# A gated cross-attention stack: first-attention scores in four row groups, biases folded, one-operation rounding

## The reference

```python
x = x + tanh(g_xattn[0]) * L0_xattn(layernorm(x), ctx)   # 16 heads of 16, softmax over 361 context rows, then W1, relu, W2
x = x + tanh(g_ffn[0])   * L0_ffn(layernorm(x))          # top-1 mixture of 8 experts
x = x + tanh(g_xattn[1]) * L1_xattn(layernorm(x), ctx)   # ternary weights, int8 activations
x = x + tanh(g_ffn[1])   * L1_ffn(layernorm(x))          # 16 experts project q, k, v; attention inside each batch
```

## Time and profile before

| what | us |
|---|---|
| median of three runs (lowest, highest) | 641.66 (640.87, 642.61) |
| the profiled execution's own time | 640.18 |
| its span | 638.4 |
| PE busy in the span | 591.8 (93%) |
| DVE busy | 325.1 (51%) |
| ACT busy | 219.7 (34%) |
| POOL busy | 72.1 (11%) |

### The profile page before, as it was taken

One profiled execution on the slowest core, in us unless ns is written; L12 is line 12 of the kernel. 1 busy time (PEld: TensorE's weight loads), 2 busy tenths in 40 slices (PEclk: granted clock), 3 DMA queues, 4 the chain that ended last, 5 costly groups with the idle time before them and its releaser, 6 DMA issues.

```text
span 638.4 us, 9303 instructions
## 1 busy us (share of the span) xinstructions
PE 591.8 (93%) x3611; PEld 393.6 (62%) x3611; DVE 325.1 (51%) x772; ACT 219.7 (34%) x511; POOL 72.1 (11%) x69
## 2 busy tenths in 40 slices
PE   6989999999999889999998399777899999999996
PEld 4756444444556769999996267547465555555653
DVE  3696767588668451121221877777742223222542
ACT  2644655646663461112214454482210000000100
POOL 0053200000008011223221000000100100000000
PEclk9999999999999878999999699886999999999999
DMA  8900000100003634999991000600633743230000
GB/s 203 344 17 1 16 2 1 35 2 3 1 2 101 217 112 164 328 338 361 322 358 61 22 0 1 232 2 0 198 108 99 265 140 96 78 99 1 0 27 26
DMA packets 25195, 69.93 MB, mean 110 GB/s; under 512 B 5143, under 2 KB 12919, under 8 KB 21319
## 3 DMA queue, kind: packets, MB, share of 16 engines
q1 hardware_dynamic: 21798, 58.16, 27.6%
q0 software_dynamic: 3360, 11.28, 5.2%
HBM read 64.62 MB, written 4.80 MB: 109 GB/s over the span
## 4 chain that ended last, share of the span: by engine, by line
PE 87%; DVE 5%; ACT 3%; DMA 2%; issue 1%; POOL 1%; SPq 0%; DVEq 0%; ACTq 0%; POOLq 0%
PE bank L2035 20%; PE bank L1559 12%; PE bank L1877 8%; PE bank L1890 8%; PE bank L1706 7%; PE bank L2071 7%; PE bank L1680 5%; PE bank L1724 3%; PE bank L1934 2%; PE bank L1649 2%; PE bank L1957 2%; PE bank L1712 2%; ACT region L1458 1%; PE bank L1960 1%; PE bank L1947 1%
## 5 line engine op out<-in xcount | busy, mean ns | idle before, releaser
L2035 PE MATMUL bank<-region,kvT 128*128 128x400 f32 x384 | 130.4, 500 | 1.0 <-DVE region L1138 1.0
L2035 PEld LDWEIGHTS bank<-region,kvT 128*128 128x128 f32 x384 | 72.4, 190 | 55.5 <-issue 1.6
L1144 DVE TENSOR_TENSOR region<-xT,stage 128x800 f32<-128x800 f32 x30 | 29.7, 992 | 69.7 <-PE bank L2035 69.5
L714 DVE TENSOR_REDUCE nmax<-bank 100x2 f32<-100x722 f32 x64 | 55.2, 905 | 15.1 <-PE bank L1680 14.7
L1877 PEld LDWEIGHTS bank<-stage,region 128*128 128x128 f32 x448 | 54.7, 200 | 1.6 <-issue 0.9
L1877 PE MATMUL bank<-stage,region 128*128 128x128 f32 x448 | 55.0, 283 | 0.5 <-ACT stage L1393 0.5
L1890 PE MATMUL bank<-region,stage 128*128 128x256 f32 x224 | 50.7, 379 | 0.0
L1890 PEld LDWEIGHTS bank<-region,stage 128*128 128x128 f32 x224 | 41.5, 190 | 5.1
L2071 PE MATMUL bank<-region,kvt 128*128 128x400 f32 x128 | 43.9, 500 | 0.0
L916 DVE TENSOR_SCALAR stage<-bank,stage 128x128 f32<-128x128 f32 x56 | 15.8, 344 | 52.0 <-PE bank L1877 52.0
L1706 PE MATMUL bank<-xT,kvt 64*121 64x400 f32 (+1 forms) x144 | 38.9, 543 | 1.5 <-ACT kvT L1372 0.6
(11 more groups left out here) (337 smaller groups left out, 899.9 us busy)
## 6 DMA issues: line engine op xcount, KB each, us to landing
region<-in_e_w SPq DMA_DIRECT2D x28, 1024.0 KB, 5.2
kvT<-in_p_qkv SPq DMA_DIRECT2D x32, 384.0 KB, 3.1
stage<-w_dram POOLq DMA_DIRECT2D x2, 1600.0 KB, 12.9
stage<-in_t_f SPq DMA_DIRECT2D x1, 2048.0 KB, 14.7
kvt<-in_p_o SPq DMA_DIRECT2D x1, 2048.0 KB, 8.8
stage<-in_e_b SPq DMA_DIRECT2D x14, 128.0 KB, 7.2
region<-in_ctxT SPq DMA_DIRECT2D x3, 541.5 KB, 13.5
stage<-w_dram POOLq DMA_DIRECT2D x1, 1200.0 KB, 9.4
```

Source lines behind the costliest of these rows:

```text
L714: dve.tensor_reduce(nmax[:, b % 2, at_h:at_h + 9:8], banks[0:N, bank:bank + 2, 0:M], AX.X, ALU.max, negate=True)\
L1144: dve.tensor_tensor(x_w[n % NW], xT[:, :, at_h], w_bc[h][:, None, e, :].to_broadcast([P, 2, HT]), ALU.mult).then_inc(S["xw_done"], 1)
L2035: ins = pe.matmul(psum[3 * h + j][:, 0:HT], p_w[n % NP][:, k, j * HE:(j + 1) * HE], x_w[n % NW][:, k, :], start=e == 0 and k == 0, stop=e ...
```

## The change

It has five parts.

1. **Scores in quads.** The six pairs of a batch become three *quads*, `score_quad(n, c)`: first four bf16 matmuls of 32 rows and 400 columns that add the maxima (L1756 of the changed kernel), then twice four f32 matmuls of 32 rows and 200 columns (L1760), two heads to a row group. `qm` has half the columns, and POOL writes 400 elements a partition instead of 800.
2. **Banks.** Waves and quads take four banks each from a ring of six (banks 0 to 5). `bank_pair_free` makes a group wait, two banks at a time: the second two wait for the first two of the group just before it (for a wave its first reduce, for a quad its second exponential). nm and all chain units share one bank (6), and each waits until ACT has emptied the one before.
3. **Order.** The table `STEP` sets it for PE and ACT: wave 3 is now last but the turn, and wave (n+1, 0) stands behind nm(n), not ahead of it.
4. **Biases.** b_att is folded into the bias of the text layer and into the sum of the two halves, so L1960 is gone, and so are DVE's reciprocal and two products for its row; three small DVE operations are new. 
5. **f2 and a context layer.** One operation scales an input and adds 128, and its write to bf16 rounds it (DVE takes 5 and 3 of the 8 blocks, ACT the others); PE takes 128 times the sum of the weights off again with one more matmul a batch, for which DVE sums the f2 weights behind the expert loop. Context layer 5 is moved ahead of the expert loop.

```diff
-OWN = (0, 3, 6)
+OWN = (5, 3)
+OFFSET = 128.0
...
-FIRST = [0]
-UNIT, CHAIN, TOTAL = {}, {}, {}
-TOP_TURN, TOP_SPREAD, LARGE_SUM = (3, 5), (3, 9), (4, 7)
+CHAIN_BANK, RING = 6, 6
+STEP = (("nm",), ("wave", 0), ("chain", 0), ("quad", 0), ("heads",), ("chain", 1), ("wave", 1), ("chain", 2),
+        ("values", 0), ("quad", 1), ("chain", 3), ("wave", 2), ("chain", 4), ("values", 1), ("quad", 2),
+        ("chain", 5), ("wave", 3), ("turn",))
+TOP_TURN, TOP_SPREAD, LARGE_SUM = (3, 2), (3, 5), (4, 3)
...
+def ring_bank(g, i):
+    return (4 * g + i) % RING
...
-                pool.tensor_tensor(qm[b % 3], qT[:, :, None, b * N:(b + 1) * N].to_broadcast([P, 2, 4, N]),
-                                   const("quadmask")[:, None, :, None].to_broadcast([P, 2, 4, N]),
+                pool.tensor_tensor(qm[b % 3], qT[:, :, None, b * N:(b + 1) * N].to_broadcast([P, 2, 2, N]),
+                                   const("pairmask")[:, None, :, None].to_broadcast([P, 2, 2, N]),
                                    ALU.mult).then_inc(S["qm_done"], 1)
...
                     dve.wait_ge(S["x_mm"], 2 * (4 * b + w) + h + 1)
-                    at_h = 4 * (w % 2) + 2 * h + w // 2
-                    bank = 2 * h + (4 if b == 0 else 0)
-                    dve.tensor_reduce(nmax[:, b % 2, at_h:at_h + 9:8],
+                    bank = 2 * h + 4 if b == 0 else ring_bank(GROUP["wave", b, w], 2 * h)
+                    dve.tensor_reduce(nmax[:, b % 2, 4 * w + 2 * h:4 * w + 2 * h + 2],
                                       banks[0:N, bank:bank + 2, 0:M], AX.X, ALU.max, negate=True)\
                         .then_inc(S["x_max"], 1)
...
+            dve.tensor_scalar(scol[:, 34:35], att[:, 1:2], -0.2, None, ALU.mult)
+            link(dve.tensor_tensor(scol[:, 31:32], att[:, 0:1], att[:, 1:2], ALU.add))
+            dve.scalar_tensor_tensor(scol[:, 32:34], scol[:, 31:32].to_broadcast([P, 2]), 0.1,
+                                     cols[:, COLS["txt"]:COLS["txt"] + 2], ALU.mult, ALU.add)
...
-            dve.wait_ge(S["consts_in"], 16)
-            link(dve.reciprocal(v_scale[:, 2:4], scol[:, 43:45]))
-            for a in range(2):
-                ins = dve.tensor_scalar(bias_row[0:1, a * P:(a + 1) * P], rows[0:1, 512 + a * P:512 + (a + 1) * P],
-                                        v_scale[0:1, 2 + a:3 + a], None, ALU.mult)
-            ins.then_inc(S["v_scale"], 1)
...
+            dve.memset(offset, -OFFSET)
+            link(dve.tensor_reduce(f2_total, weight("f2").rearrange("p (k n) -> p n k", k=8), AX.X, ALU.add))
+            dve.tensor_copy(f2_sum, f2_total).then_inc(S["f2_sums"], 1)
...
-                                  cols[:, 14 + m:15 + m], ALU.mult, ALU.add).then_inc(S["f_out"], 1)
+                                  scol[:, 32 + m:33 + m], ALU.mult, ALU.add).then_inc(S["f_out"], 1)
...
-                dve.tensor_tensor(fsum[:, at_b], fT[:, 0, at_b], fT[:, 1, at_b], ALU.add).then_inc(S["fsum_done"], 1)
+                dve.scalar_tensor_tensor(fsum[:, at_b], fT[:, 0, at_b], scol[:, 34:35], fT[:, 1, at_b], ALU.add, ALU.add)\
+                    .then_inc(S["fsum_done"], 1)
...
                 at_h = slice(h * HT, (h + 1) * HT)
-                if m in OWN:
-                    link(dve.tensor_scalar(h1T[:, m, at_h], h1T[:, m, at_h], scol[:, 23:24], None, ALU.mult))
-                else:
-                    dve.wait_ge(S["act_scaled"], 2 + 5 * h + len([k for k in range(m + 1) if k not in OWN]))
-                dve.tensor_scalar(q1T[:, m, at_h], h1T[:, m, at_h], MAGIC, MAGIC, ALU.add, ALU.subtract)\
+                dve.tensor_scalar(q1T[:, m, at_h], h1T[:, m, at_h], scol[:, 23:24], OFFSET, ALU.mult, ALU.add)\
                     .then_inc(S["q1_done"], 1)
...
+
+            def quad_out(n, c):
+
+                rows_c, g = CH[c][1], GROUP["quad", n, c]
+                for i in range(4):
+                    act.wait_ge(S["y_mm_a"], UNIT[n, c, i] + 1)
+                    act.activation(probsT[n % 2][0:rows_c, c, i].rearrange("p w n -> p (w n)"),
+                                   psum[ring_bank(g, i)][0:rows_c, 0:4 * N], ACT.Exp).then_inc(S["y_out_a"], 1)
...
-            for b in range(5):
+            for b in range(6):
                 last_context_out(b)
...
             for h in range(2):
-                for m in range(8):
-                    if m not in OWN:
-                        act.mul(h1T[:, m, h * HT:(h + 1) * HT], h1T[:, m, h * HT:(h + 1) * HT], scol[:, 23:24])\
-                            .then_inc(S["act_scaled"], 1)
+                at_h = slice(h * HT, (h + 1) * HT)
+                for m in range(OWN[h], 8):
+                    act.activation(q1T[:, m, at_h], h1T[:, m, at_h], ACT.Identity, bias=scol[:, 35:36],
+                                   scale=scol[:, 23:24]).then_inc(S["act_scaled"], 1)
...
-                pe.wait_ge(S["y_out_a"], y - 2)
+                pe.wait_ge(S["y_out_a"], LAST_CHAIN[y] + 1)
                 for k in range(2):
-                    ins = pe.matmul(psum[4 + y % 3][:, 0:M], w[:, k, m * P:(m + 1) * P], qc[0:rows_k, k, b, :],
+                    ins = pe.matmul(psum[CHAIN_BANK][:, 0:M], w[:, k, m * P:(m + 1) * P], qc[0:rows_k, k, b, :],
                                     start=k == 0, stop=k == 1)
                 ins.then_inc(S["y_mm_a"], 1)
...
+            def bank_pair_free(g, e):
+
+                pair = 2 * g + e - RING // 2
+                if pair < 0:
+                    return
+                kind, b, at_u = USER[pair // 2]
+                if kind == "wave":
+                    pe.wait_ge(S["x_max"], 2 * (4 * b + at_u) + pair % 2 + 1)
+                else:
+                    pe.wait_ge(S["y_out_a"], UNIT[b, at_u, 2 * (pair % 2) + 1] + 1)
+
...
+                    if b == 0:
+                        bank = 4 + i
+                        if (w, i) == (1, 2):
+                            pe.wait_ge(S["sum_read"], 1)
+                        if w > 0 and i % 2 == 0:
+                            pe.wait_ge(S["x_max"], 2 * (w - 1) + i // 2 + 1)
+                    else:
+                        bank = ring_bank(GROUP["wave", b, w], i)
+                        if i % 2 == 0:
+                            bank_pair_free(GROUP["wave", b, w], i // 2)
...
-            def score_pair(b, u):
-
-                c, t = u // 4, u // 2 % 2
-                (c0, rows_c), y0 = CH[c], UNIT[b, u]
-                bank = [psum[4 + (y0 + g) % 3][0:rows_c, 0:4 * N] for g in range(2)]
-                for g in range(2):
-                    if y0 + g >= 3:
-                        pe.wait_ge(S["y_out_a"], y0 + g - 2)
-                    at_g = slice(64 * g, 64 * g + 64)
-                    pe.matmul(bank[g], kT[at_g, t, b, c0:c0 + rows_c],
-                              qm[b % 3][at_g, t].rearrange("p j n -> p (j n)"), start=True, stop=False)
-                if u == 0:
+            def score_quad(b, c):
+
+                (c0, rows_c), g = CH[c], GROUP["quad", b, c]
+                bank = [psum[ring_bank(g, i)][0:rows_c, 0:4 * N] for i in range(4)]
+                if c == 0:
                     pe.wait_ge(S["y_out_a"], FIRST[b] + 1)
-                for g in range(2):
-                    at_g = slice(64 * g, 64 * g + 64)
-                    pe.matmul(bank[g], rows_bf[at_g, t, 0:rows_c], nmT[b % 2][at_g, :],
-                              start=False, stop=True).then_inc(S["y_mm_a"], 1)
+                for i in range(4):
+                    if i % 2 == 0:
+                        bank_pair_free(g, i // 2)
+                    at_i = slice(32 * i, 32 * i + 32)
+                    pe.matmul(bank[i], rows_bf[at_i, 0:rows_c], nmT[b % 2][at_i, :], start=True, stop=False)
+                for t in range(2):
+                    for i in range(4):
+                        at_i = slice(32 * i, 32 * i + 32)
+                        ins = pe.matmul(bank[i][:, 2 * N * t:2 * N * t + 2 * N], kT[at_i, t, b, c0:c0 + rows_c],
+                                        qm[b % 3][at_i, t].rearrange("p j n -> p (j n)"), start=False, stop=t == 1)
+                        if t == 1:
+                            ins.then_inc(S["y_mm_a"], 1)
...
+            pe.wait_ge(S["x_max"], 8)
+            for n in range(B):
+                for kind, *at_u in STEP:
+                    if kind == "nm":
+                        turn_maxima(n)
+                    if kind == "wave" and n + 1 < B:
+                        score_wave(n + 1, at_u[0])
+                    if kind == "chain" and at_u[0] < len(EXTRA[n]):
+                        chain_unit(*EXTRA[n][at_u[0]])
+                    if kind == "chain" and (n, at_u[0]) in TOTAL:
+                        total_unit(n, at_u[0])
+                    if kind == "quad":
+                        score_quad(n, at_u[0])
+                    if kind == "heads" and n >= 2:
+                        turn_heads(n - 2)
+                    if kind == "values" and n >= 1:
+                        values(n - 1, 2 * at_u[0])
```

(28 more changed lines are left out.)

203 lines of the change are left out of this document (95 added, 108 removed).

## The result

| | us |
|---|---|
| changed kernel, median of 4 runs (lowest, highest) | 654.81 (651.34, 660.52) |
| kernel before beside it, median of 4 | 642.02 (640.87, 642.61) |
| ratio, 95% interval | 1.021 (1.013 to 1.029) |
| the profiled execution, its span | 656.5, 654.7 |

The change makes the kernel 2.1% slower. The forecast was 656 (637 to 668). The page of the changed kernel: span, PE's busy time and its share, PE's busy tenths and granted clock in 40 slices, the chain that ended last. The earlier trace rows answers to it.

What follows compares the result with a forecast made beforehand. PE bounds the kernel now; waits would take over in the first attention loop. Terms +12.4 (loop), +9 (clock), -1.05, -6.2, -0.8, +1.0 make +14.35 on 640.18, so 654.5; the median 1.5 above: 656 us (637 to 668).

Steps and rivals of the forecast that it cites:

- The tail on DVE: First attention loop: PE stands still ahead of each nm for DVE's reduces and split, about 2.9 us, 2.1 or 3.2.
- the walk: First attention loop followed batch by batch at full clock: seven batches take 122.5 us against 108.6, +13.9.
- Waits inside a batch: First attention loop: PE waits for ring banks and, at chain units 2 and 4, about 1 us each for ACT.
- the throughput of ACT or DVE would bound the loop: First attention loop, by the skill's rule: ACT and DVE bound at 78.91 and 92.13 of 131.90 us; a gain remains.
- The clock: First attention loop: waits ahead of nm drop PE to half clock in five of seven batches, about 1.8 us each, +9.
- The start: Ahead of nm(0): PE's wait for POOL's first spread goes, -1.05 us, and one wave fewer, 0.8 us.
- The term for POOL: POOL's first spread, with half the elements, ends 1.6 us earlier, so PE's wait for it goes: -1.05 us.
- The second attention loop: Second attention loop: without the bias product of 0.39 us, 16 steps shrink from 2.14 to 1.75 us, -6.2.
- f2: f2 products: extra matmuls cost 0.8 us a half, one-operation rounding lets PE begin about 1.6 earlier; together -0.8, bounds -2 and +1.
- Context layer 5: Ahead of the expert loop: ACT ends the added layer at 239.4, past PE's earlier start at 238.41, costing +1.0 us.
- Nothing comes back: Behind the expert loop: moving context layer 5 returns no time, since PE waits there for the gather anyhow.
- the faster rival: First attention loop: evictions keep up, only the tail remains, loop -9.5 us, median 625; chance 0.16.

Runs made afterwards that it cites:

- e1: Changed kernel with wave 3 moved behind chain unit 4, ahead of values 1: 647.59 us, ratio to the kernel before 1.010.
- e6: Changed kernel with DVE's split put ahead of the last two chain maxima: 651.06 us, ratio to the kernel before 1.014.
- e2: Changed kernel with five unused f32 matmuls on PE ahead of each nm but the first: 644.63 us, ratio to the kernel before 1.0049.
- e10: Kernel before with one unused DVE maximum over 4800 columns ahead of each split but the first: 664.90 us, ratio 1.040.
- e8: Kernel before with only context layer 5 moved ahead of the expert loop: 640.54 us, ratio 0.999.
- e9: Changed kernel with another STEP order (values and a quad behind wave 3) and the split ahead of the last two chain maxima: 625.97 us, ratio to before 0.975.
- e4: Kernel before with all parts outside the first attention loop (folded biases, f2, context layer 5): 631.59 us, ratio 0.983.
- e7: Kernel before with the folded biases alone: 633.51 us, ratio 0.989.

## Why the prediction was right, step by step

**The tail on DVE.** Right in place and nearly in size: 2.2 to 3.7 us ahead of six nm's, 1.5 ahead of the one of batch 4, 17.7 in sum; the walk had 2.9, 2.1 and 3.2. e1 shortens it and gains 7 us; e6 shortens it too, with a gain that is not clear of the scatter.

**Waits inside a batch.** Right: chain units 7.9 us in all, and 8.8 in e2 at full clock; the ring's first reduce up to 0.8, the second exponential up to 0.4 a time. The sum of the seven at full clock was 122.5 by the walk and 122.9 in e2. Batch by batch e2 has 15.5, 17.7, 17.0, 17.8, 16.4, 19.8 and 18.6: six are within 0.3 of the walk, and the fourth is 1.4 longer, because the added matmuls themselves waited for ACT there and ran past the end of the split. That the throughput of ACT or DVE would bound the loop can be left aside: in the 135.5 us of the seven batches they were busy 66.3 and 78.6.

**The clock.** Right in kind, undersized: this is the term of the sum that was furthest off. +9 was said, and 135.5 - 122.9 = 12.6 is what e2 gives back. The last batch comes on top, for which the sum had nothing: from nm(7) to second_layer(0) it took 23.9 us at 0.86, and 21.7 in e2 at full clock, where 21.8 was said. Together 14.8. In the seven batches the clock fell six times, where I had counted five: at 75.6, 99.5, 116.6, 137.0, 157.5 and 178.0, each time in the wait ahead of an nm or less than 0.8 us behind it. It stayed at 0.50 for 3.4 to 13.7 us, 8.0 on average, where 7 was said, and a fall cost 1.1 to 3.9 us, 2.1 on average, where 1.8 was said. That one price for all came out so near is luck in part. The cause is shown by e2 and e10: PE's standing still, not the quads; how long a wait it takes is not (see e1, e6, e8, e9 and e10). The scatter of the changed kernel is the clock's as well: its four runs had spans of 649.5, 651.3, 654.7 and 658.7 us at 0.926, 0.919, 0.915 and 0.905.

**The start.** nm(0) came 2.5 us earlier; said were 1.05 and the wave's 0.8. The wave came as said. The term for POOL was wrong in size: with half the elements the first spread took 2.63 us instead of 3.28, 0.65 less and not 1.6, and PE still waited 0.43 for it.

```profile
39.24 2.63 POOL L485 TENSOR_TENSOR xT<-xn,consts 128x400 f32<-128x400 f32 x1 [6.98 <-issue]
```

The other 1.08 us are that it began at 39.24 instead of 40.32. That is no work of the change: in kernels that have the old spread it begins between 38.99 (e4) and 40.77 (e7).

**The second attention loop.** The step was mis-sized: not 2.14 - 0.39 = 1.75 but 1.58, as PE's rows of one step of the changed kernel show.

```profile
410.60 0.77 PE L1981 MATMUL bank<-kvT,stage 128*100 128x361 f32 x2
...
411.21 0.46 PE L1994 MATMUL bank<-consts,stage 100*121 100x100 f32 x3
...
411.50 0.83 PE L2004 MATMUL bank<-stage,kvt 121*128 121x100 f32 x6
...
412.17 0.77 PE L1981 MATMUL bank<-kvT,stage 128*100 128x361 f32 x2
```

From 410.60 to 412.17 is 1.57. Scores to turns took 0.69 and takes 0.61, the values to what follows them took 0.77 and takes 0.67: a product of one row, with a weight load of its own, cost more than the 0.39 to its successor. DVE, which had 1.71 of a step, did not hold PE up: PE shows no wait in these steps. But DVE is now busy 1.54 of 1.58, so little more was to be had. From the loop's start to f1 it is 40.5 and 32.8 us: -7.7, not -6.2, and not 16 x 0.56 = 9.0 either. Only ten steps are full ones; they give 5.6, the five ahead of them 0.1 (0.8 us of them at half clock now) and what is behind them 2.0.

**f2.** From f1's start to the last stage's first projection, 42.4 and 41.9 us: -0.5 against -0.8. Within the bounds given.

**Context layer 5.** This step was wrong, in size and in sign, and what it got right is only where the wait is. PE's first work of the expert loop waited 0.9 us for ACT's copy of that layer,

```profile
264.39 0.44 PE L1909 MATMUL bank<-consts,stage 128*128 128x128 f32 x2 [0.92 <-ACT kvt L1437]
```

but it had waited 2.03 for the tokens before, and from second_layer(0) to the loop it is 42.9 and 43.0 us: +0.1, not +1.0. ACT's part was priced too high: behind nm(7) its last copy ended at 64.24 before and at 65.48 in e8, 1.24 later and not 2.15.

"Nothing comes back" was wrong as well. The expert loop gives 2.8 us: before, it began at half clock (0.50 from 238.5 to 245) behind the wait of 2.03; after, it had 1.00 from the start, behind the 0.9. It took 106.0 us in the kernel before and 106.1 in e7 and e10, which leave the layer where it was, and 103.2 to 104.8 in the changed kernel and the other nine experiments, which all move it. Behind the loop another 0.9 comes back, 11.95 to 11.08 from the context layers to the first layernorm turn. ACT's saved layer is not the reason, since DVE waits for the experts' rows in both:

```profile
350.91 0.88 DVE L936 SCALAR_TENSOR_TENSOR x<-stage,top_w,x 100x256 f32<-100x256 f32 x2 [6.56 <-DMA stage<-y_slots]
```

```profile
373.21 0.88 DVE L960 SCALAR_TENSOR_TENSOR x<-stage,top_w,x 100x256 f32<-100x256 f32 x2 [1.78 <-DMA stage<-y_slots]
```

They stand 6.50 us behind the loop's end before and 5.63 after; why the rows come sooner no run shows, and at the start of the second attention loop nothing of it is left (24.6 and 24.7 us). In e8's total all this does not show: its expert loop took 103.2 us as well, but the clock fell once more in its first loop, and from the second attention loop on its profiled execution took 4.0 us longer than that of the kernel before.

**What no step had.** The last stage took 1.3 longer, and the clock fell once more near its start, at 468.1. So the +14.35 met the +16.3 partly because errors cancelled: up to second_layer(0) 5.5 too low (+20.35 against +25.9), from there to the second attention loop 3.6 too high, that loop 1.5 too high, the rest 1.6 too low. The first of these is the clock's 5.8 and 0.4 of the walk, less 0.7 at the start. The forecast of the median has luck in it too: it was set 1.5 above the profiled execution, and the median came out 1.7 below it. Three slips of the arithmetic changed little: 24.7 less seven tails of 2.2 is 9.3 and not 9.5, half of the faster rival's gain gives 633 and not 635, and the chances of the cases add up to 0.98.

## What to carry to other kernels

Packing TensorE tighter moves the bound to the handovers. Before the edit, walk one iteration on every engine with the gaps from the trace; here that gave seven batches within 0.4 us at full clock, and another order of the same operations turned 2.1% slower into 2.8% faster (1.7% of it from the parts outside the loop). A wait in each iteration costs its length and can then cost the clock: look at what the granted clock does behind the idle stretches that are already in the trace, and if the wait can't be removed, PE work in its place can pay (e2, -10 us).

## What the hardware showed that I had not expected

- Five useless matmuls in each wait made the kernel 10 us faster.
- No length of a wait decides whether the clock falls. It stayed at 1.00 behind 1.73 us in e10 and behind 1.44 in e1; it fell behind 1.33 in e1, behind 1.48 in e6, and behind 0.59 and 0.75 in e9. Behind the same waits of 0.28 and 0.50 it fell in e8 and e4 and stayed up in the kernel before.
- Moving context layer 5 alone (e8) left a wait of 0.9 instead of 2.03 us ahead of the expert loop, and the loop, now at full clock from its start, took 2.8 us less. That the shorter wait is the reason fits the rest and was not tested by itself.
- Half the elements were not half the time on POOL: 2.63 us instead of 3.28 for the first spread.
- In e6 one fall lasted 30 us with PE busy 92% of it; in the dense loop of e10 the clock was back at 1.00 some 7 us after a fall (79.4 to 86.2).
- A one-row product in an f32 sequence cost 0.56 us a step, 0.17 more than the distance to its successor.
